# One subtraction moved by one mask on VectorE, and the layernorms' epsilon added on GpSimd

## The reference

```python
h = _layernorm(x) * (1 + ca) + sa                  # layernorm "a" of the kernel
q, k, v = jnp.split(h @ Wqkv.T + bqkv, 3, axis=-1)
q = (elu(q) + 1 + FEAT_EPS) / sqrt(E);  k = elu(k) + 1 + FEAT_EPS
num = einsum(q, cumsum(k v));  den = einsum(q, cumsum(k)) + FEAT_EPS
out = (num / den) @ Wout.T + bout
x = x + ga * (_layernorm(out) * gamma + beta)      # layernorm "c", model 0
h = _layernorm(x) * (1 + cb) + sb                  # model 1
# _L0_ffn_ref(h): begins with a layernorm (model 2), then its q, k, v,
# softmax attention, and for each token the one expert of eight that its gate chooses
```

## Time and profile before

| | before |
|---|---|
| median of 3 runs | 707.77 us (707.38 to 709.08) |
| span of the profiled execution | 705.1 us |
| mean granted TensorE clock | 0.970 |
| PE busy | 629.5 us (89%) |
| DVE busy | 609.4 us (86%) |
| ACT busy | 494.0 us (70%) |
| POOL busy | 418.5 us (59%) |

### The profile page before, as it was taken

The page is one execution under the profiler, slowest core; times in us unless marked ns, Lnnn a source line. Parts: engine busy times, 40 slices in busy tenths (PEclk is TensorE's granted clock), DMA queues, the critical chain, the costliest instruction groups (busy, mean ns, idle before and its releaser), DMA issues.

```text
span 705.1 us, 16639 instructions
## 1 busy us (share of the span) xinstructions
PE 629.5 (89%) x5448; PEld 323.9 (46%) x5448; DVE 609.4 (86%) x1566; ACT 494.0 (70%) x1007; POOL 418.5 (59%) x931
## 2 busy tenths in 40 slices
PE   4599689889887798899999999999999999899994
PEld 2366566666555322222323323233333322498994
DVE  6878999998977898899999999999999995686552
ACT  3634656766645347888888888888898889855662
POOL 6212666575656457135676787887777872566553
PEclk9899999999999959999999999999999999999997
DMA  6664133243263313016430120302103001456600
GB/s 180 176 215 122 49 111 108 97 158 106 92 203 98 89 46 110 26 54 202 121 91 2 58 69 13 113 25 87 39 19 109 25 12 35 138 171 175 173 31 12
DMA packets 42900, 66.26 MB, mean 94 GB/s; under 512 B 7948, under 2 KB 36335, under 8 KB 39808
## 3 DMA queue, kind: packets, MB, share of 16 engines
q1 hardware_dynamic: 39232, 56.73, 26.8%
q0 software_dynamic: 3296, 8.41, 3.3%
q10 hardware_dynamic: 288, 0.07, 0.0%
HBM read 41.64 MB, written 22.26 MB: 91 GB/s over the span
## 4 chain that ended last, share of the span: by engine, by line
PE 51%; DVE 20%; ACT 17%; issue 6%; POOL 3%; DMA 1%; SPq 1%; ACTq 0%; POOLq 0%; DVEq 0%
PE bank L1081 11%; ACT arena L2000 10%; PE pair L1070 7%; DVE arena L1569 6%; PE bank L1042 6%; PE pair L1331 4%; DVE arena L1402 4%; PE pair L1340 2%; PE bank L1340 2%; DVE arena L1431 2%; PE bank L1092 2%; PE bank L936 2%; ACT arena L1969 2%; PE bank L925 2%; DVE arena L1552 1%
## 5 line engine op out<-in xcount | busy, mean ns | idle before, releaser
L2000 ACT ACTIVATE arena<-pair 128x512 f32<-128x512 f32 x506 | 278.1, 602 | 50.5 <-PE pair L1070 48.6
L1569 DVE TENSOR_REDUCE arena<-bank 128x1 f32<-128x512 f32 x388 | 251.3, 682 | 7.5 <-PE bank L1042 6.5
L1070 PE MATMUL pair<-q_stack,k_stack 64*128 64x512 bf16 x506 | 158.0, 386 | 5.9 <-ACT arena L2000 5.3
L1042 PE MATMUL bank<-k_stack,q_stack 63*128 63x512 bf16 x388 | 137.4, 395 | 8.6 <-DVE arena L1569 4.8
L1081 PE MATMUL bank<-arena,values 128*9 128x512 f32 x1024 | 134.7, 598 | 1.6 <-ACT arena L2000 1.5
L1402 DVE TENSOR_TENSOR arena<-bank,cst 128x512 f32<-128x512 f32 x128 | 82.1, 682 | 15.6 <-PE bank L910 15.1
L1569 DVE TENSOR_REDUCE arena<-pair 128x1 f32<-128x512 f32 x124 | 84.3, 680 | 1.5 <-PE pair L1042 1.1
L1042 PEld LDWEIGHTS bank<-k_stack,q_stack 63*128 63x128 bf16 x388 | 33.3, 93 | 109.6 <-DVE arena L1569 24.9
L715 POOL TENSOR_TENSOR arena<-arena 128x32 f32<-128x32 f32 (+6 forms) x312 | 68.8, 220 | 24.4
L1070 PEld LDWEIGHTS pair<-q_stack,k_stack 64*128 64x128 bf16 x506 | 40.6, 93 | 48.6 <-ACT arena L2000 26.4
L1914 ACT ACTIVATE arena<-bank,den_eps 128x512 f32<-128x512 f32 x32 | 21.7, 677 | 41.2 <-PE bank L936 41.2
(11 more groups left out here) (301 smaller groups left out, 1262.0 us busy)
## 6 DMA issues: line engine op xcount, KB each, us to landing
softmax_parts<-arena SPq DMA_DIRECT2D x8, 768.0 KB
q_stack<-softmax_parts SPq DMA_DIRECT2D x48, 128.0 KB, 2.9
k_stack<-softmax_parts SPq DMA_DIRECT2D x48, 128.0 KB, 3.0
linear_parts<-arena SPq DMA_DIRECT2D x7, 768.0 KB, 3.7
q_stack<-linear_parts SPq DMA_DIRECT2D x42, 128.0 KB, 2.9
k_stack<-linear_parts SPq DMA_DIRECT2D x42, 128.0 KB, 2.9
arena<-in_L_ffn_w_dram SPq DMA_DIRECT2D x16, 256.0 KB, 4.5
v_all<-token_rows SPq DMA_DIRECT2D x20, 192.5 KB, 2.7
```

The source lines that it names most:

```text
L1042: pe.matmul(bank[:], qs[b % 2][rows, slot, qt * P:(qt + 1) * P], ks[b % 2][rows, slot, :], start=True, stop=True).then_inc(d_s_m, 1)
L1070: pe.matmul(score_bank(s)[:], ks[u][rows, 2 * g + x, kt * P:(kt + 1) * P], qs[u][rows, 2 * g + x, :], start=True, stop=True).then_inc(d_s_ ...
L1569: dve.reduce_max(mx[:, m % 2, col:col + 1], bank[:], AX).then_inc(d_s_mr, 1)
L2000: act.activation(pt[:, kt % 2, x, half, :], score_bank(s)[:], ACT.Exp, scale=SCALE).then_inc(d_s_e, 1)
```

## The change

Two edits, independent of each other.

1. DVE's `a_rest(s + 2, 0)`, the query's rest, stood in unit 6 behind the key's feature. It now stands in unit 7, directly behind `masked(g)` and ahead of `normalise` and `output`. The key's rest stays where it was, behind `output` in unit 7. In steps -2 and -1 no mask of unit 7 exists yet; there the order hardly changes. In steps 0 to 5 the query's rest and the mask change places.
2. The addition of the epsilon to the variances (`tensor_scalar` on four columns) and the wait for bn_aggr in front of it leave DVE's `stats`. GpSimd's `a_rstd` and `c_rstd` wait for bn_aggr instead, do the addition themselves, then turn the mean's sign, and wait for their own addition before the power. The end of the kernel has a similar sequence of its own (`end_stats`), which is not touched.

```diff
@@ gpsimd
                 def a_rstd(a):
-                    pool.wait_ge(a_s_ve, a + 1)
+                    pool.wait_ge(a_s_mv, C * (a + 1))
+                    pool.tensor_scalar(a_ve[:], a_mv[:, :, 1], LN_EPS, None, ALU.add).then_inc(a_s_ve, 1)
                     wait(pool, a_s_xn, a)
                     pool.tensor_scalar(a_nm[:], a_mv[:, :, 0], -1.0, None, ALU.mult).then_inc(a_s_nm, 1)
+                    pool.wait_ge(a_s_ve, a + 1)
                     pool.tensor_tensor(a_rs[:], a_ve[:], k.halfneg[:], ALU.pow).then_inc(a_s_rs, 1)
...
                 def c_rstd(b, m):
+                    pool.wait_ge(c_s_mv[m], C * (b + 1))
+                    pool.tensor_scalar(c_ve[:, m, :], c_mv[:, m, :, 1], LN_EPS, None, ALU.add).then_inc(c_s_ve[m], 1)
+                    pool.tensor_scalar(c_nm[:, m, :], c_mv[:, m, :, 0], -1.0, None, ALU.mult).then_inc(c_s_nm[m], 1)
                     pool.wait_ge(c_s_ve[m], b + 1)
-                    pool.tensor_scalar(c_nm[:, m, :], c_mv[:, m, :, 0], -1.0, None, ALU.mult).then_inc(c_s_nm[m], 1)
                     pool.tensor_tensor(c_rs[:, m, :], c_ve[:, m, :], k.halfneg[:], ALU.pow).then_inc(c_s_rs[m], 1)
@@ vector, stats
                     for c in range(C):
                         dve.bn_aggr(mv[:, c, :], st[:, c, :]).then_inc(s_mv, 1)
-                    dve.wait_ge(s_mv, C * (b + 1))
-                    dve.tensor_scalar(ve, mv[:, :, 1], LN_EPS, None, ALU.add).then_inc(s_ve, 1)
@@ vector, the loop over units
                         if unit(g) and g:
                             masked(g)
+                        if d == 7 and has(s + 2):
+                            a_rest(s + 2, 0)
                         if d % 2 == 1 and chunk((g - 3) // 2):
                             normalise((g - 3) // 2)
...
                             a_feature(s + 2, 1)
                             if s == -1:
                                 masked(0)
-                            a_rest(s + 2, 0)
                         if d == 7 and has(s + 2):
                             a_rest(s + 2, 1)
```

More of the change, by code:

```diff
@@ L1427, in output, with stats @@
                     dve.tensor_tensor(tile(k.v_all, q // C, q % C), b_oy[:, 0:P], k.BO, ALU.add).then_inc(s_yc, 1)
-                def stats(src, b, st, mv, ve, s_st, s_mv, s_ve, s_nb):
+                def stats(src, b, st, mv, s_st, s_mv, s_nb):
                     for c in range(C):
@@ L1526, in a_stats @@
                     dve.wait_ge(w_s_x[min(a, 2)], 16 if a < 2 else 16 * 3)
-                    stats(k.x_all, a, a_st, a_mv, a_ve[:], a_s_st, a_s_mv, a_s_ve, a_s_nb)
+                    stats(k.x_all, a, a_st, a_mv, a_s_st, a_s_mv, a_s_nb)
                 def c_stats(b, m):
@@ L1535, in c_stats @@
                         dve.wait_ge(c_s_h, b + 1)
-                    stats((k.v_all, k.x_all, k.h_all)[m], b, c_st[:, m], c_mv[:, m], c_ve[:, m, :],
-                          c_s_st[m], c_s_mv[m], c_s_ve[m], c_s_nb[m])
+                    stats((k.v_all, k.x_all, k.h_all)[m], b, c_st[:, m], c_mv[:, m],
+                          c_s_st[m], c_s_mv[m], c_s_nb[m])
                 def a_relu(a, z):
```

## The result

The kernel after takes 713.57 us (median of 4 runs, 712.39 to 714.94) against 708.03 us (707.38 to 709.08) for the kernel before beside it: ratio 1.0074, 95% interval 1.006 to 1.0087. The forecast was 706.9 us in a range up to 709.9; the time lies above it. The medians are 5.5 us apart. The two profiled executions are 7.8 us apart, with spans of 712.9 and 705.1 us: each is one execution, after's is one of its longer ones (714.7 us), and before's has a clock of 0.970, where the median of 25 further runs on the same chip is 0.965. In every run the clock tells the two kernels apart: 0.954 to 0.958 in the four of after, 0.960 to 0.972 in those 25.

The account below looks back on a forecast made before the run. It saw an apparent DVE bound, with the query's rest held up by GpSimd's SBUF use, but ACT close behind. Terms summed to -0.83 us: span 705.1 to 704.3, plus 2.67 to the median gives 706.9 us, range 702.8 to 709.9.

Parts of the forecast that it names:

- Step 0, +1.19: In step 0, without x_ready, the move only puts the mask before the query's rest, delaying PE's turn: +1.19 us.
- the sum: All terms over the whole kernel added together: -0.83 us, taking the span from 705.1 to 704.3 us.
- Steps 1 to 5, the collision: The query's rest no longer stands still for GpSimd's x_ready; by step -0.5, -0.16, +0.2, -0.16, -1.0 us.
- that +0.2: Step 3: PE's products run slowly, so mask 7 and the moved rest come later: +0.2 us.
- near 26.4: Expected sign in the linear stage: steady steps, 26.58 us before, would take near 26.4 us.
- The statistics on VectorE: -0.02 for the chain: Epsilon's addition moved to GpSimd leaves the chain through GpSimd unchanged (-0.02 us); DVE saves 0.19 us per call.
- Rival (c): Changed gaps make two or three more steps run at the lower clock, 0.43 us each: 708.5 us; chance 0.17 for worse.
- GpSimd in steps 6 and 7, +0.1: Where GpSimd is late, in c_rstd of model 0, the addition costs about 0.05 us: +0.1 for both steps.
- The softmax's start, -0.5: Around the softmax's start, three statistics calls ahead of DVE work that is last save 0.19 us each: -0.5 us.
- Rival (a): DVE's saving in the linear stage arrives whole, 1.09 us in five steps: 703.0 us, outer bound about 696; chance 0.18.
- Rival (b): GpSimd's last part beats the key's rest, which stands still; steps lose about 0.3 us: 710.1 us; chance 0.1.

Follow-up runs that it names:

- e1: The kernel before with only the query's rest moved behind mask 7 in steps 0 to 5, epsilon still on VectorE; 708.62 us, ratio 1.0017.
- e8: The kernel before with the query's rest moved from step 1 on, plus unread PE products in steps 0 to 5; 719.66 us, ratio 0.9972.
- e5: Control: the kernel before with unread PE products before the turns and in unit 6, steps 0 to 5; 721.19 us, ratio 0.9983.
- e2: The kernel after with the query's rest put back, leaving only the epsilon on GpSimd; 712.29 us, ratio 1.0049 against before.
- e7: The kernel before with only the epsilon moved to GpSimd, plus unread PE products before turns and in unit 6, steps 0 to 5; 722.59 us, ratio 0.9996.
- e4: The kernel after with unread PE products before turns and in the gap of unit 6, steps 0 to 5; 707.48 us, ratio 0.9987 against before.
- e9: The kernel before with three unread 16-column copies on ACT behind c_normed of model 0, lengthening the gap of unit 6, unfilled; 724.67 us, ratio 1.0036.
- e10: The kernel before with the query's rest moved behind mask 7 in steps 1 to 5, nothing filled; 722.07 us, ratio 0.9986.
- e3: The kernel after with the query's rest moved only from step 1 on, not in step 0; 710.51 us, ratio 1.0039 against before.
- e12: The kernel before with the epsilon on GpSimd, added behind the mean's negation, plus unread PE products in steps 0 to 5; 725.04 us, ratio 1.003.

## Where the prediction was right and wrong

**Step 0, +1.19: right.** The rest starts behind both masks, and the table has +1.19 from 40.1 to 62.2 in e1. In after the turn at 58.61 is 1.76 late (0.56 of it from ahead of step 0), so +1.20; its idle time went from 0.80 to 2.17 us. That such a wait can cost the clock too was not in the sum: the turn a few us later is 3.19 late.

**Steps 1 to 5, the collision: right in mechanism, too small in size.** The rest takes 0.68 us (0.69 at most) in all eight steps, and the other arm decides what is left of it. The e8 row less the e5 row, two kernels with the same filling and no fall in steps 1 to 5, gives by step -0.75, -0.21, -0.23, -0.24, -1.02, where I had -0.5, -0.16, +0.2, -0.16, -1.0. In e8 the turn of step 1 comes 0.16 us later first, as worked out, and then gives back more. The mis-sized terms are step 1 and step 3. For step 3 I had the lower clock meet the late rest. In e8 there was no lower clock there, but after shows it in steps 2 and 4: the clock fell there in after and in e2, which differ by the moved rest alone, and after loses 0.48 and 0.29 us more than e2. So the sign of that +0.2 was right, for every step in which the clock falls.

**The two edits aren't independent in time.** The sum added the gain of the moved rest to that of the statistics. The moved rest alone brings a steady step from 26.59 us to 26.33 in e1 and 26.36 in e8, as forecast ("near 26.4"), and the epsilon alone to 26.52 in e7. Both together give 26.56 in e4, and 26.57 in after's own step at the full clock: the gain of the move is gone. Which wait takes it back wasn't followed.

**The statistics on VectorE: -0.02 for the chain was wrong.** Before: DVE's last aggregates, then GpSimd.

```profile
122.36 0.28 DVE L1436 BATCH_NORM_AGGREGATE arena<-arena 128x2 f32<-128x6 f32 x3
```

```profile
122.93 0.23 POOL L649 TENSOR_SCALAR arena<-arena 128x4 f32<-128x4 f32 x1 [1.00 <-DVE arena L1438]
123.12 1.04 POOL L650 TENSOR_TENSOR arena<-arena,halfneg 128x4 f32<-128x4 f32 x1
```

After, the same place:

```profile
127.63 0.28 DVE L1440 BATCH_NORM_AGGREGATE arena<-arena 128x2 f32<-128x6 f32 x3
```

```profile
128.00 0.24 POOL L651 TENSOR_SCALAR arena<-arena 128x4 f32<-128x4 f32 x1 [1.29 <-DVE arena L1440]
128.32 0.23 POOL L652 TENSOR_SCALAR arena<-arena 128x4 f32<-128x4 f32 x1
128.51 1.03 POOL L654 TENSOR_TENSOR arena<-arena,halfneg 128x4 f32<-128x4 f32 x1
```

From the end of the aggregates to the power it was 123.12 - 122.64 = 0.48 us, and is 128.51 - 127.91 = 0.60: +0.12. I had taken 0.19 us from one small instruction to the next, from the pair at 122.93; that is the distance from a TENSOR_SCALAR to the power, in both kernels. From one TENSOR_SCALAR to the next it is 0.32.

**The step that failed: what the two small terms do to PE's idle time.** PE's products of that unit follow VectorE's mask, which follows the aggregates; they start 124.10 - 122.64 = 1.46 us after the aggregates before and 129.14 - 127.91 = 1.23 after the change, since VectorE is rid of the addition:

```profile
124.10 0.40 PE L910 MATMUL bank<-q_stack,k_stack 63*128 63x128 bf16 x8 [0.19 <-DVE arena L1402]
```

```profile
129.14 0.40 PE L914 MATMUL bank<-q_stack,k_stack 63*128 63x128 bf16 x8
```

So PE is done 0.23 us earlier, and what it then waits for, through GpSimd's power and ACT, comes 0.12 later (from the power to the end of the gap it is 126.81 - 123.12 = 3.69 us before and 132.19 - 128.51 = 3.68 after): 1.51 + 0.35 is the 1.85 us of the gap, to within the rounding. The gain was real on VectorE and arrived on PE as idle time in front of a later arm. In the forecast's sum such idle time, and the clock behind it, stand at nothing; that is what put the time above the range. Rival (c) had this mechanism, with two or three more steps at 0.43 us and about 0.4 for the late rest each, and a total of 708.5. The price of a step was near (0.96 and 1.13 us in steps 4 and 2, after's row beside e4's). It was too low in the number of falls and in the long ones: the clock fell at six places from 56 to 235 us (twice as long at two of them, 77 and 223), together 7.9 us by e4. I had used the idle of 1.51 us in every step with one fall as the sign that falls are rare, and never worked out what the edits would make of that idle time.

**GpSimd in steps 6 and 7, +0.1: too small.** e7 against e5 between 194.4 and 229.6 is +0.88 us, with a filled unit 6 in the steps ahead. By the turns of e7 beside those of before, 0.38 of it comes between 199 and 206 us, 0.10 by 218 and 0.40 by 230. The wait is GpSimd's. From the end of its last part in step 6 to the power of model 0 it was 201.80 - 201.50 = 0.30 us before and is 201.77 - 201.18 = 0.59 in e7, so 0.29 for which I had 0.05; PE's gap behind it, in front of `before`, goes from 1.13 to 1.41 us.

**The softmax's start, -0.5: about right.** From 229.6 to the end of the span after goes from +8.52 to +7.8, e2 from +5.83 to +5.4, e4 from +0.88 to +0.6; e1, which leaves the addition on VectorE, from +1.29 to +1.5.

**Rival (a), the whole saving: false.** A step at the full clock takes 26.57 us, not 25.6, and a steady step of e1 26.33. The freed time is waiting, as these rows of DVE in after show (seam of steps 2 and 3):

```profile
108.35 0.68 DVE L1554 TENSOR_TENSOR arena<-fq_all,arena 128x512 f32<-128x512 f32 x1
...
109.64 0.68 DVE L1554 TENSOR_TENSOR arena<-arena 128x512 f32<-128x512 f32 x1
110.54 1.29 DVE L1406 TENSOR_TENSOR arena<-bank,cst 128x512 f32<-128x512 f32 x2 [0.22 <-PE bank L914]
112.23 0.69 DVE L1564 TENSOR_TENSOR arena<-pair,arena 128x512 f32<-128x512 f32 x1 [0.40 <-ACT arena L1987]
```

**Rival (b), the collision moves: false, by the 0.13 us foreseen.** The same rows: the key's rest starts 109.64 - 109.03 = 0.61 us after the query's ends (worked out: 0.60). GpSimd's timeline has the last part 0.13 behind it:

```profile
109.77 1.57 POOL L646 TENSOR_TENSOR arena<-arena 128x512 bf16<-128x512 f32 x1 [2.88 <-ACT arena L1959]
```

VectorE is first and keeps its 0.68 us; it is GpSimd that takes 1.57 instead of 1.16. The Trainium skill, "SBUF — State Buffer", section "Who interferes with whom", would have the one that issues first hold the pair for its whole instruction; in both directions the trace agrees in who is held (VectorE 1.77 us before, GpSimd 1.57 after). How long is nearly so: VectorE stood 1.09 us of the 1.22 that GpSimd still had to run, GpSimd 0.41 of the 0.55 that VectorE had.

Without the falls of the clock in steps 0 to 5 the kernel after is what e4 shows. By the medians that is 0.13% faster than before, 0.9 us, and near the -0.83 of the sum; by the traces it is 0.6 us slower (705.7 against 705.1). By e4's turns steps 1 to 5 give -1.98 us, of which 0.43 is the fall that before had, so -1.55 against -1.62 forecast; but by other parts: -0.67, -0.01, -0.02, -0.03 and -0.82, and steps 6 and 7 cost +0.89 where +0.1 stood. That the medians come so near the sum is partly luck. What the edits give at the full clock is small either way, and the falls decided the result.

## What to carry to other kernels

An engine that is 86% busy can be relieved of 11 us and PE gets only idle time for it, if another arm sets when PE goes on. So for each saving work out what becomes of PE's longest idle times, not only of its end. Here, with PE near 90% busy, a gap that grew from 1.51 to 1.85 us brought falls of the clock, mostly of 0.7 us a step (up to 1.6 where the rest was moved too, nothing in step 1 of e9), and together they cost more than the edit could give. Move an instruction only in the steps where it collides (here from step 1 on). Unused products in a gap that couldn't be closed brought the time back here, as long as they were no more than it holds. And look at the clock of every run, not only at that of the traced one.

## What was unexpected of the hardware

- At the gap of unit 6 the clock fell in 1 of 5 steps (before), 0 of 5 (e1) and 1 of 5 (e10) where it is 1.5 us, and in 4 of 5 (after), 5 of 5 (e2), 4 of 5 (e3) and 4 of 5 (e9) where it is 1.82 to 1.86. Of gaps of 2.22 us it fell behind one of two (e1); at the 2.36 us near 218 it held in e4. These are counts of one traced execution each. What else decides stays open. e1's spread of 8.4 us between runs goes with the clock of each run; where in them it fell isn't known, as only one has a trace.
- The clock was also low from 22 to 28 us, from 35 to 39 us and from 243 to 264 us in the kernel before, and at nearly the same times in e4. That was not worked on.
- On GpSimd a TENSOR_SCALAR of 128x4 starts 0.32 us after another, though each is recorded with 0.23 or 0.24; the power starts 0.19 after one, and 0.31 if it waits for what that one wrote (e12). Why the two distances differ stays open.
- The second and third chip take 14 us longer for the kernel before. The linear stage takes the same there; the time comes between 625 and 647 us, in the experts' part. Its cause wasn't looked for. No time of a whole kernel is compared across chips but by ratio; the table compares turns of the linear stage.
